# Smaller first weights, earlier x, copies ahead of exponentials, gathers in PSUM and denominators by transposition in a one-core transformer block

## The reference

```python
def cross(q, ctx):                          # q = layernorm(x); one head of width 512
    qp, kp, vp = q @ Wq.T + bq, ctx @ Wk.T + bk, ctx @ Wv.T + bv
    attn = softmax(qp @ kp.T / sqrt(32))    # 512 x 8192
    return (attn @ vp) @ Wo.T + bo
def linear(x):                              # linear attention, 16 heads of 32
    q, k, v = split(x @ W_qkv); q, k = relu(rmsnorm(q) * qn), relu(rmsnorm(k) * kn)
    kv = k.T @ v per head; out = (q @ kv) / (q @ sum(k) + 1e-6)
    return out @ W_out + b_out
def ffn(x):                                 # 8 experts, top 2 by sigmoid scores: 4 gated MLPs
    ...                                     # of width 256, 2 identities, 1 relu, 1 zero
    return routed + causal_conv(x, 4 taps) + conv_b
x = x + cross(layernorm(x), ctx); x = x + linear(layernorm(x)); x = x + ffn(layernorm(x))
```

## Time and profile before

| | |
|---|---|
| median of the runs | 541.64 us |
| the profiled execution | 541.28 us, span 539.2 us |
| busy: TensorE, VectorE, ScalarE, GpSimd | 531.7, 357.8, 253.0, 201.2 us |
| ScalarE, 128x512: cast of Wv, `keep`, Exp into `ph`, Exp into a bank | 0.61, 0.59, 0.63, 0.59 us |
| ScalarE: cast of 128x1024 (ct, cn), table load | 1.05, 1.28 us |
| VectorE: subtraction of 128x512 (xT), `bn_stats`, aggregate, variance, reciprocal, shift | 0.69, 0.69, 0.18, 0.15, 0.16, 0.21 us |
| GpSimd, 128x512: cast of Wo, subtraction | 0.84, 1.29 us |

### The profile page before, as it was taken

One profiled execution on the slowest core, in us unless ns is written; L12 is line 12 of the kernel. 1 busy time (PEld: TensorE's weight loads), 2 busy tenths in 40 slices (PEclk: granted clock), 3 DMA queues, 4 the chain that ended last, 5 costly groups with the idle time before them and its releaser, 6 DMA issues.

```text
span 539.2 us, 6788 instructions
## 1 busy us (share of the span) xinstructions
PE 531.7 (99%) x2458; PEld 439.8 (82%) x2458; DVE 357.8 (66%) x605; ACT 253.0 (47%) x412; POOL 201.2 (37%) x132
## 2 busy tenths in 40 slices
PE   8999999999999999999999999999999999999997
PEld 7788788788888888888888888788887888888886
DVE  5574656784668685648898556999665427638757
ACT  4743334764444554445436544457355452551210
POOL 4625050432113212341147324347337959800000
PEclk9999999999999999999999999999999999999999
DMA  8611232232322232424222311252420314200002
GB/s 322 286 52 58 86 111 85 84 151 101 135 79 78 85 138 91 156 82 148 82 79 78 119 39 41 78 174 101 156 79 1 117 40 141 95 1 0 1 0 80
DMA packets 14865, 51.60 MB, mean 96 GB/s; under 512 B 1776, under 2 KB 1776, under 8 KB 14192
## 3 DMA queue, kind: packets, MB, share of 16 engines
q1 hardware_dynamic: 14832, 51.16, 26.7%
HBM read 50.11 MB, written 1.05 MB: 95 GB/s over the span
## 4 chain that ended last, share of the span: by engine, by line
PE 91%; DVE 3%; issue 2%; ACT 2%; POOL 1%; DMA 1%; SPq 0%; DVEq 0%; POOLq 0%; ACTq 0%
PE bank L1276 26%; PE bank L1346 10%; PE bank L1347 10%; PE bank L1348 10%; PE bank L1357 10%; PE bank L1358 10%; PE bank L1359 10%; PE bank L1266 1%; POOL w_v_l L490 1%; DMA wo_raw<-wo_t 1%; PE bank L1476 1%; PE bank L1485 1%; DVE ring L991 0%; DVE parts_max L910 0%; DVE psum_keys L1014 0%
## 5 line engine op out<-in xcount | busy, mean ns | idle before, releaser
L504 POOL TENSOR_TENSOR cn_l<-raw_n,cn_h 128x1024 fp32r<-128x1024 f32 x32 | 81.1, 2534 | 198.6 <-ACT cn_h L650 198.6
L945 DVE TENSOR_TENSOR top<-top,bank 128x512 f32<-128x512 f32 x60 | 41.2, 686 | 91.0 <-ACT ring L668 90.6
L1346 PE MATMUL bank<-qk_h,ct_h 128*128 128x512 f32 x256 | 100.3, 392 | 0.7 <-DVE top L945 0.7
L1357 PE MATMUL bank<-ph,cn_h 128*128 128x512 f32 x256 | 99.9, 390 | 0.9 <-DVE pl L1000 0.5
L1348 PE MATMUL bank<-qk_h,ct_l 128*128 128x512 f32 x256 | 99.6, 389 | 0.0
L1359 PE MATMUL bank<-ph,cn_l 128*128 128x512 f32 x256 | 99.6, 389 | 0.0
L1358 PE MATMUL bank<-pl,cn_h 128*128 128x512 f32 x256 | 99.6, 389 | 0.0
L1347 PE MATMUL bank<-qk_l,ct_h 128*128 128x512 f32 x256 | 99.6, 389 | 0.0
L668 ACT COPY ring<-bank 128x512 f32<-128x512 f32 x64 | 37.5, 586 | 82.3 <-PE bank L1348 82.3
L675 ACT ACTIVATE ph<-ring 128x512 fp32r<-128x512 f32 x64 | 40.4, 632 | 67.7 <-PE bank L1359 48.0
L991 DVE TENSOR_TENSOR ring<-ring,shift_b 128x512 f32<-128x512 f32 x64 | 58.7, 922 | 0.0
(11 more groups left out here) (218 smaller groups left out, 864.1 us busy)
## 6 DMA issues: line engine op xcount, KB each, us to landing
raw_t<-ctx_t SPq DMA_DIRECT2D x32, 512.0 KB, 4.1
raw_n<-ctx_n SPq DMA_DIRECT2D x32, 512.0 KB, 3.3
...
```

The lines of the kernel that those rows point to most:

```text
L504: pool.tensor_tensor(cn[p % CNB][1][:], raw_n[p % 2][:], cn[p % CNB][0][:].bitcast(F32), ALU.subtract).then_inc(cnl_ready, 1)
L945: dve.tensor_tensor(top[:], top[:], bank[:, S_BANKS[i % 2], :], ALU.max).then_inc(max_done, 1)
L1346: pe.matmul(bank[:, dst, :], ct[i // 2 % 2][0][:, c, keys], qk[0][:, c, :], start=(c == 0), stop=False)
L1357: pe.matmul(bank[:, c, :], keys[0][:, q % 2, d], ph[q % PB][:], start=first, stop=False)
```

## The change

The loads of chunk 0 of Wv and Wo are cut into halves of 256 columns and everything that follows them too (casts, subtractions, 12 matmuls of 256 columns, `first_part`). x 0 and x 1 load ahead of Wo 2 and Wv 2. Wo 1 is split on ScalarE and VectorE, Wq 0 is cast on GpSimd. The orders on ScalarE and VectorE change, and the four transposes of x move to later parts of the fold. The warm-up takes 7 products on `ones`. In the loop ScalarE copies the raw scores before the exponentials, those of the first tiles come one step later (`exponents_at`, `RAMP`), and a first Exp stands at step 8. `parts_max`, `block_max` and `run_max` lie in PSUM bank 7. The bias row is split in two fp32r parts. The denominators are summed on VectorE by a transposition and the gathers. Around the second norm, both halves of `w_v` are cast before it and xT's copies move. Left out below are declarations, renamed waits, and `.[:]` of the tensors in PSUM.

```diff
+RAMP = 4
...
-WARM = 10
+WARM = 7
...
-parts_max = at(173.5, "parts_max", [P, QB // 8, TB])
+small_psum = bank[:, 7, 256:512]
+parts_max = small_psum[:, 0:64].rearrange("p (g b) -> p g b", b=TB)
 shift_q = at(173.5 + 0.25, "shift_q", [P, TB])
-block_max, run_max, key_bias, biased_max = (at(173.5 + 0.3125 + n / 16, f"by_32_{n}", [QB, TB]) for n in range(4))
+block_max, run_max = (small_psum[0:QB, 64 + TB * n:64 + TB * (n + 1)] for n in range(2))
+key_bias, biased_max = (at(173.8125 + n / 16, f"by_32_{n}", [QB, TB]) for n in range(2))
...
+def exponents_at(k):
+
+    if k == RAMP:
+        return [q for q in (k + LEAD - 1, k + LEAD) if q < TILES]
+    q = k + LEAD - (k < RAMP)
+    return [q] if 0 <= q < TILES else []
...
-    def load_weights(e):
+    def load_wv(e):
         sp.dma_start(wv_raw[:, e, :], wv_in[e]).then_inc(wv_loaded[e], 16)
+
+    def load_wo(e):
         sp.dma_start(wo_raw[:, e, :], wo_t[e]).then_inc(wo_loaded[e], 16)
+
+    def load_wv0(h):
+        part = slice(h * HALF, (h + 1) * HALF)
+        sp.dma_start(wv_raw[:, 0, part], wv_in[0][:, part]).then_inc(wv0_loaded[h], 16)
+
+    def load_wo0(h):
+        part = slice(h * HALF, (h + 1) * HALF)
+        sp.dma_start(wo_raw[:, 0, part], wo_t[0][:, part]).then_inc(wo0_loaded[h], 16)
...
-    load_weights(0)
+    load_wv0(0)
+    load_wo0(0)
+    load_wo0(1)
+    load_wv0(1)
+    load_wv(1)
+    load_wo(1)
     load_x(0)
-    load_weights(1)
     load_x(1)
+    load_wo(2)
+    load_wv(2)
     load_x(2)
-    load_weights(2)
     load_x(3)
-    load_weights(3)
+    load_wo(3)
+    load_wv(3)
     for e in range(C):
         sp.dma_start(wq_raw[:, e, :], wq_t[e]).then_inc(wq_loaded[e], 16)
...
+    pool.memset(ones[:], 1.0).then_inc(ones_ready, 1)
     pool.memset(ident[:], 0.0).then_inc(ident_ready, 1)
...
-    pool.memset(ones[:], 1.0).then_inc(ones_ready, 1)
-    for e in range(1, C):
+    for e in range(2, C):
         split_wo(e)
+    pool.wait_ge(wq_loaded[0], 16)
+    pool.tensor_copy(wq[0][:, 0, :], wq_raw[:, 0, :]).then_inc(wq0_high, 1)
     for e in range(C):
-        pool.wait_ge(wq_high, e + 1)
+        if e == 0:
+            pool.wait_ge(wq0_high, 1)
+        else:
+            pool.wait_ge(wq_high, e)
         pool.tensor_tensor(wq[1][:, e, :], wq_raw[:, e, :], wq[0][:, e, :].bitcast(F32), ALU.subtract).then_inc(wq_ready, 1)
...
+    pool.wait_ge(bv_step, 2 * C - 1)
+    pool.tensor_copy(bv_parts[0][:], bv_wo[:]).then_inc(bv_high, 1)
+    pool.wait_ge(bv_high, 1)
+    pool.tensor_tensor(bv_parts[1][:], bv_wo[:], bv_parts[0][:].bitcast(F32), ALU.subtract).then_inc(bv_ready, 1)
...
-    high_wv(0)
-    act.wait_ge(wo_loaded[0], 16)
-    act.copy(wo[0][:, 0, :], wo_raw[:, 0, :]).then_inc(wo0_high, 1)
+
+    def high_wv0(h):
+        part = slice(h * HALF, (h + 1) * HALF)
+        act.wait_ge(wv0_loaded[h], 16)
+        act.copy(wv[0][:, 0, part], wv_raw[:, 0, part]).then_inc(wv0_high, 1)
+
+    def high_wo0(h):
+        part = slice(h * HALF, (h + 1) * HALF)
+        act.wait_ge(wo0_loaded[h], 16)
+        act.copy(wo[0][:, 0, part], wo_raw[:, 0, part]).then_inc(wo0_high, 1)
+
+    high_wv0(0)
+    high_wo0(0)
+    high_wo0(1)
+    high_wv0(1)
     high_wv(1)
+    act.wait_ge(wo_loaded[1], 16)
+    act.copy(wo[0][:, 1, :], wo_raw[:, 1, :]).then_inc(wo1_high, 1)
     std_of(0)
+    high_wv(2)
     apply_of(0)
     std_of(1)
-    high_wv(2)
     apply_of(1)
     std_of(2)
+    high_wv(3)
     high_xT(0, XT_BANKS)
+    std_of(3)
     apply_of(2)
-    high_wv(3)
-    std_of(3)
+    apply_of(3)
     high_xT(1, XT_BANKS)
-    apply_of(3)
-    high_wq(0)
     high_xT(2, XT_BANKS)
     high_xT(3, XT_BANKS)
     high_wq(1)
...
     for s in range(TILES + AHEAD):
         k = s - AHEAD
+        if s == 8:
+            act.activation(exp_table[:], ones[:], ACT.Exp)
         if s % 2 == 0 and 2 <= s // 2 + 1 < NP:
             high_ct(s // 2 + 1)
         if s % SB == 4 and s > 2 * SB and s // SB <= NSB:
             rescale(s // SB - 1)
-        if 0 <= k + LEAD < TILES:
-            exponents(k + LEAD)
         if s < TILES:
             keep(s)
+        for q in exponents_at(k):
+            exponents(q)
...
     for h in range(2):
         high_w2("q", h)
+    for h in range(2):
+        high_w2("v", h)
     for t in range(TT):
-        if t >= 2:
-            high_xT(2 * TT + t - 2, X1_BANKS)
         std_of(TT + t)
+        if t == 1:
+            high_xT(2 * TT, X1_BANKS)
         apply_of(TT + t)
-        if t % 2 == 0:
-            high_w2("v", t // 2)
+        if t == 1:
+            high_xT(2 * TT + 1, X1_BANKS)
     act.wait_ge(w2_ready, 2 * 2)
...
         dve.tensor_tensor(wv[1][:, e, :], wv_raw[:, e, :], wv[0][:, e, :].bitcast(F32), ALU.subtract).then_inc(wv_ready, 1)
-    low_wv(0)
-    dve.wait_ge(wo0_high, 1)
-    dve.tensor_tensor(wo[1][:, 0, :], wo_raw[:, 0, :], wo[0][:, 0, :].bitcast(F32), ALU.subtract).then_inc(wo0_ready, 1)
+    def low_wv0(h):
+        part = slice(h * HALF, (h + 1) * HALF)
+        dve.wait_ge(wv0_high, h + 1)
+        dve.tensor_tensor(wv[1][:, 0, part], wv_raw[:, 0, part], wv[0][:, 0, part].bitcast(F32),
+                          ALU.subtract).then_inc(wv0_ready, 1)
+
+    def low_wo0(h):
+        part = slice(h * HALF, (h + 1) * HALF)
+        dve.wait_ge(wo0_high, h + 1)
+        dve.tensor_tensor(wo[1][:, 0, part], wo_raw[:, 0, part], wo[0][:, 0, part].bitcast(F32),
+                          ALU.subtract).then_inc(wo0_ready, 1)
+
+    low_wv0(0)
+    low_wo0(0)
+    low_wo0(1)
+    low_wv0(1)
     low_wv(1)
+    dve.wait_ge(wo1_high, 1)
+    dve.tensor_tensor(wo[1][:, 1, :], wo_raw[:, 1, :], wo[0][:, 1, :].bitcast(F32), ALU.subtract).then_inc(wo1_ready, 1)
     first_stats(0)
+    first_stats(1)
     ln_scale(0)
-    first_stats(1)
+    low_wv(2)
     ln_scale(1)
-    low_wv(2)
     first_stats(2)
-    ln_scale(2)
-    low_xT(0, XT_BANKS)
     first_stats(3)
     low_wv(3)
+    ln_scale(2)
     ln_scale(3)
+    low_xT(0, XT_BANKS)
     low_xT(1, XT_BANKS)
     low_xT(2, XT_BANKS)
...
         n = (k + LEAD) // SB
-        if n != NSB - 2 or k + LEAD < 0:
+        if k < RAMP:
+            return k + LEAD
+        if n != NSB - 2:
             return min(k + LEAD + 1, TILES)
...
-        if 0 <= k + LEAD - 1 < TILES:
-            low_p(k + LEAD - 1)
-            add_den(k + LEAD - 1)
+        for q in exponents_at(k - 1):
+            low_p(q)
+            add_den(q)
...
             key_terms()
-        if s == 8:
+        if s == 9:
             biases()
-    dve.wait_ge(den_psum, 1)
-    dve.reciprocal(inv_den[:], bank[:, MISC, 0:TT]).then_inc(inv_ready, 1)
+    dve.wait_ge(den_done, TILES)
+    dve.wait_ge(shift_ready_q, P // QB * NSB)
+    dve.transpose(flipped[:], psum_keys[:]).then_inc(inv_step, 1)
+    dve.wait_ge(inv_step, 1)
+    dve.reduce_sum(parts_max[:, 0, :], flipped[:].rearrange("p (b k) -> p b k", k=QB), AX.X).then_inc(inv_step, 1)
+    dve.wait_ge(inv_step, 2)
+    gather_parts(inv_step, 2)
+    dve.reduce_sum(block_max, parts_max[0:QB].rearrange("p g b -> p b g"), AX.X).then_inc(inv_step, 1)
+    dve.wait_ge(inv_step, 6)
+    dve.reciprocal(run_max, block_max).then_inc(inv_step, 1)
+    dve.wait_ge(inv_step, 7)
+    for g in range(P // QB):
+        dve.tensor_copy(inv_den[g * QB:(g + 1) * QB, :],
+                        run_max.rearrange("p (t g) -> p g t", g=P // QB)[:, g, :]).then_inc(inv_ready, 1)
...
-        if t == 2:
-            low_xT(2 * TT, X1_BANKS)
+        if t >= 2:
+            low_xT(2 * TT + t - 2, X1_BANKS)
         dve.wait_ge(x1_ready, t + 1)
         ln_stats(TT + t)
         ln_scale(TT + t)
-    low_xT(2 * TT + 1, X1_BANKS)
...
         return w[0][:, c, a:b], w[1][:, c, a:b]
-    pe.wait_ge(ident_ready, 2)
-
     def warm(products):
+        some = ones[:].to_broadcast([P, P])
         for n in range(products):
-            pe.matmul(bank[:, 7, 0:P], ident[:], ident[:], start=True, stop=True)
+            pe.matmul(bank[:, 3, 0:P], some, some, start=True, stop=True)
+
+    pe.wait_ge(ones_ready, 1)
...
-    transposed_at = {(1, 2): 0, (2, 0): 1, (2, 2): 2, (3, 1): 3}
-    for e in range(C):
-        pe.wait_ge(wv_ready, e + 1)
-        if e == 0:
-            pe.wait_ge(wo0_ready, 1)
+    def first_part(c, h, k):
+
+        a = wv[(0, 1, 0)[k]][:, 0, c * P:(c + 1) * P]
+        b = wo[(0, 0, 1)[k]][:, 0, h * HALF:(h + 1) * HALF]
+        pe.matmul(bank[:, WVO_BANKS[c], h * HALF:(h + 1) * HALF], a, b, start=(h == 0 and k == 0),
+                  stop=False)
+
+    for h in range(2):
+        if h == 0:
+            pe.wait_ge(wv0_high, 1)
+        pe.wait_ge(wo0_high, h + 1)
+        for k in range(3):
+            if k == 1 and h == 0:
+                pe.wait_ge(wv0_ready, 1)
+            if k == 2:
+                pe.wait_ge(wo0_ready, h + 1)
+            for c in range(2):
+                first_part(c, h, k)
+    pe.wait_ge(wv0_ready, 2)
+    for c in range(2, C):
+        fold_part(0, c)
+
+    transposed_at = {(2, 1): 0, (2, 3): 1, (3, 1): 2, (3, 3): 3}
```

(29 more changed lines are left out.)

35 lines of the change are left out of this document (25 added, 10 removed).

## The result

| | before | changed kernel |
|---|---|---|
| median of 4 runs each, same chip | 541.61 us (541.52 to 542.23) | 538.49 us (538.17 to 538.62) |
| ratio, 95% interval | | 0.9938 [0.9926, 0.9951] |
| profiled execution | 541.28 us, span 539.2 | 538.51 us, span 536.7 |

The kernel is 0.6% faster, 3.1 us. The forecast was 537.5, in a range of 535.9 to 539.9: the time is inside it, 1.0 us above the forecast.

The account below looks back on a forecast made before the run. TensorE, busy 99% of the span, was taken to bound the kernel. Terms +0.1 - 0.4 - 0.9 - 1.25 - 0.9 - 0.8 = -4.15 us; 541.28 - 4.15 = 537.13, plus 0.36 = 537.5 us; 8-in-10 range 535.9 to 539.9.

Parts of the forecast that it names:

- The likeliest case: Whole kernel: the forecast itself, 537.5 us, chance 0.52.
- Bias row: fp32 bias product after the loop's early steps: two fp32r products take 0.46 instead of 0.86 us, -0.40, bounds -0.5 to 0.
- Start: First matmul to Q projection: earlier fold given back in waits, +0.1 us, between -1.2 and +0.8; Q projection at 19.3 to 20.3.
- The three waits: TensorE gaps before fold chunk 1, chunk 2 and the Q projection: 0.6, 0.9 and 1.4 us.
- the start pays: Rival, fold: statistics and casts do not hold chunk 2, last transposes at 16.9, 1.2 us more gained, 536.3; chance 0.12.
- Gathers: Last block: 32x16 copies in PSUM remove TensorE's waits for `pl` and the accumulator, -1.25 us, bounds 0 and -1.4.
- denominators: Loop's end: eight TensorE instructions go, VectorE's chain stays hidden by 0.4 us; -0.9 us, bounds -1.0 and -0.3.
- second norm: Before `w_k` and `w_v`: TensorE's waits go with earlier casts and xT copies, -0.8 us, bounds -0.9 and +0.3.
- Ramp: Loop, near 102.63 us: raw scores copied first ends TensorE's wait for the running maximum, -0.9 us, bounds -1.1 to 0.
- The gaps stay: Rival, loop: copies not the cause or ScalarE's order shifts the wait; 1.25 and half of 0.9 remain, 539.1; chance 0.18.
- only the removed matmul time counts: Rival, whole kernel: 0.4 + 0.8 us go, waits return elsewhere, the start costs 0.8: 541.2; chance 0.11.
- The clock: Slower rival, fold: gaps keep TensorE at 1.2 GHz, 547 us, or 542.5 if half of the work runs so; chance 0.07.

Follow-up runs that it names:

- the first trace: Profiled execution of the changed kernel, no further edit, against that of the kernel before: 538.51 us, span 536.7.
- the late split: Changed kernel, only with GpSimd waiting for the fourth low context part (step 4) before it splits the bias row: 537.43 us, ratio 0.9930.
- Both pairs of medians: New start against the start of before: 538.49 and 538.33 us in the changed kernel, 537.43 and 537.27 with the bias row split from step 4 on.
- the last experiment: Changed kernel with x 2 and x 3 transposed earlier, bias row split from step 4, and x 1 loaded behind Wo 2 and Wv 2: 537.29 us, ratio 0.9913.
- the first four experiments: Changed kernel with old start, chunk 0 loaded whole, last transposes earlier, or bias row split later: 538.33, 538.77, 537.08, 537.43 us; kernel before beside them 541.63.
- the end undone: Changed kernel with denominators summed by TensorE again and the old ScalarE and VectorE orders around the second norm: 540.04 us, ratio 0.9959.
- the undone exponentials: Changed kernel with exponentials ahead of the raw-score copy again and the first tiles' not a step later: 540.43 us, ratio 0.9974.
- the undone gathers: Changed kernel, only with parts_max, block_max and run_max back in SBUF: 540.63 us, ratio 0.9979.

## Why the prediction was right, and where it was off

The likeliest case was the one that came, 1.0 us short of its gain. That it came so close is partly luck: two losses of 0.65 and 1.3 us that were not in the sum were half made good by stages that gained 1.1 us more than counted. Step by step:

- **Bias row: the step that failed.** "The split adds a cast and a subtraction (2.1 us) to GpSimd, which afterwards only waits for this result. Bounds -0.5 to 0." The product itself is right (steps 5 to 7 gained 0.7 us in the first trace and 0.42 with the late split, the 0.40 of the sum; the rest of the 0.7 are small waits of these steps that the stall at step 4 covered). What I left out is who else works while GpSimd does. A pass on an engine off the critical path was counted by its own duration; its price was paid by VectorE's two-input pass beside it, 2.31 instead of 1.22 us, and TensorE paid 1.3 for that. Net the edit lost. The late split shows it: -1.06 us. The upper bound should have been about +1.0: the -0.4, and the 1.4 by which a VectorE subtraction of 2.11 us beside GpSimd exceeds the 0.69 of an undisturbed one.
- **Start: mis-sized.** The sum had +0.1. Both pairs of medians give +0.16, but spans and traces give +0.6 to +0.75, so the agreement of the times is luck. The three waits stood where they were put. The sign "the Q projection at 19.3 to 20.3" failed in every trace with this start (20.44 to 21.33). The step that was off are the landings, and in every execution traced, not in one: with the changed kernel's order Wv 1 landed at 5.45 to 6.61 us (counted 5.1), Wo 2 at 8.81 to 9.68 (counted 8.1), Wv 2 at 9.48 to 10.34 (counted 8.8). The prediction's 0.69 us a piece holds from the fifth piece to the ninth; by the same rows the first five came (6.82 - 3.24) / 4 = 0.90 apart. And two pieces fewer ahead of Wo 2 were counted as 1.5 us; between the traces with the old order (9.54 to 10.28) and the new they brought 0.5 by the medians. Why is open. The first trace alone would have put the whole miss here (+1.5), and wrongly: with the same loads the wait ahead of chunk 1 was 0.4 in one execution and 1.4 in another. The rival "the start pays" needed the last transposes earlier, and the experiment with them earlier gave that gain, 1.4 us.
- **Gathers** -1.44 for -1.25, **denominators** -0.95 for -0.9, **second norm** -0.87 for -0.8: right in place and cause, undone by themselves or, for the last two, together, with the gap back where it was. The gathers' 0.2 more is the second gap behind the copies, which went entirely. **Ramp** -1.2 for -0.9: right in place, and the order on ScalarE is shown as a cause for 0.65 of it; the rest is not shown.
- **The gaps stay** and **only the removed matmul time counts**: no old wait behind the start came back.
- **The clock.** It did not decide: the pace rose at 5.8 us in both kernels, though TensorE starts at 0.89 instead of 1.52, and the median execution shows 1.00. The mechanism exists, though. In the last experiment 0.63 for 4.5 us; in one of four executions of the late split 0.996 and 2.2 us more than the others. The prediction gave it a chance of 0.07, as a rival that could come and was not likely.
- **The sum and the median.** The traces' sum at the last matmul is -2.5 and the spans' -2.5. The median span is 536.2 us; that of the kernel before was 539.5 beside the first four experiments. The difference, -3.3, is made up of the start at its usual cost (+0.75), step 4 (+1.35) and the stages behind (-5.3); the medians of the times differ by 3.1. So the missing 1.0 us is not the step 4 wait alone, though its experiment gave 1.06. The prediction's own range for the sum, 536.2 to 538.6, does not follow from its terms either: with +0.8 for the start the upper end is 538.2, and the measured 538.49 lies above that. *Open*: what happens outside of the span. It is 2.1 to 2.3 us in every run of the kernel before, 1.84 to 1.95 with the end undone, and 1.8 to 3.6 in the changed kernel and most of its variants. More semaphores are not it. Nor was it settled why the undone exponentials cost more than their gap, and for the undone gathers only one execution shows it (its last store).
